# The corrected threshold of each score group, made by VectorE instead of GpSimd

## What is computed

```python
dots = jnp.einsum('bhid,bhjd->bhij', q, k) * QK_SCALE
dots = jnp.einsum('hg,bgij->bhij', W_pre_th, dots)        # heads are mixed
dots = jnp.where(causal[None, None], mask_value, dots)
top = jax.lax.top_k(dots, TOPK)[0]                        # TOPK = 64
vk = top[..., -1:]
dots = jnp.where(dots < vk, mask_value, dots)
attn = jax.nn.softmax(dots, axis=-1)
attn = jnp.einsum('hg,bgij->bhij', W_post_th, attn)       # and mixed again
out = jnp.einsum('bhij,bhjd->bhid', attn, v)
```

## Time and profile before

| | |
|---|---|
| median of three runs | 2098.49 us |
| the profiled execution | 2098.69 us, span 2096.9 us |
| PE busy | 1952.4 us, 93% of the span |
| VectorE busy | 1668.8 us, 80% |
| ScalarE busy | 1612.7 us, 77% |
| GpSimd busy | 862.8 us, 41% |
| granted TensorE clock, mean | 0.981 |

### The profile page before, as it was taken

The page is one execution under the profiler, slowest core; times in us unless marked ns, Lnnn a source line. Parts: engine busy times, 40 slices in busy tenths (PEclk is TensorE's granted clock), DMA queues, the critical chain, the costliest instruction groups (busy, mean ns, idle before and its releaser), DMA issues. The chain is left out here.

```text
span 2096.9 us, 56133 instructions
## 1 busy us (share of the span) xinstructions
PE 1952.4 (93%) x16059; PEld 1292.3 (62%) x16060; DVE 1668.8 (80%) x7716; ACT 1612.7 (77%) x4412; POOL 862.8 (41%) x2675
## 2 busy tenths in 40 slices
PE   7996789999999999999999999999999999996997
PEld 3433456676667666766676677666766776674433
DVE  6355389978997899789978997999699969985335
ACT  4553489978997899789968996899689978963554
POOL 3000454455445544554454445544554455421000
PEclk9997899999999999999999999999999999998998
DMA  5002012301230222122211221122112211213002
GB/s 170 26 1 95 12 33 53 79 18 45 61 73 18 62 55 60 26 54 68 45 33 48 68 48 29 48 68 48 29 48 68 48 26 46 66 45 95 0 1 80
DMA packets 113228, 104.78 MB, mean 50 GB/s; under 512 B 34449, under 2 KB 110865, under 8 KB 112913
## 3 DMA queue, kind: packets, MB, share of 16 engines
q1 hardware_dynamic: 108000, 96.65, 18.6%
q10 hardware_dynamic: 4912, 4.46, 0.7%
HBM read 19.14 MB, written 12.71 MB: 15 GB/s over the span
## 5 line engine op out<-in xcount | busy, mean ns | idle before, releaser
L1076 PEld LDWEIGHTS bankC<-R,E 128*128 128x128 f32 x2560 | 319.9, 192 | 49.7 <-issue 17.6
L1060 PE MATMUL bankB<-raw,mixpre 128*128 128x76 f32 (+37 forms) x1024 | 334.5, 421 | 13.6 <-DMA raw<-SC 12.3
L1076 PE MATMUL bankC<-R,E 128*128 128x128 f32 x2560 | 333.9, 277 | 11.5 <-POOL R L1452 11.5
L1557 DVE TENSOR_SCALAR_CACHE_REDUCE S<-S,minus_thr 128x68 f32<-128x68 f32 (+56 forms) x456 | 232.9, 511 | 110.9 <-POOL minus_thr L1436 110.1
L1427 POOL TENSOR_TENSOR S<-S,diagmask 128x8 f32<-128x8 f32 x512 | 120.2, 238 | 395.4 <-ACT S L1284 360.4
L1284 ACT ACTIVATE S<-bankB,aim_first 128x68 f32<-128x68 f32 (+56 forms) x456 | 227.3, 506 | 57.8 <-PE bankB L1060 56.9
L1452 POOL TENSOR_SCALAR R<-mixpost,rinv 128x128 f32<-128x128 f32 x512 | 199.3, 402 | 101.1 <-DVE rinv L1591 99.0
L1310 ACT ACTIVATE E<-S,nmax 128x12 f32<-128x12 f32 (+56 forms) x512 | 238.8, 523 | 0.0
L1060 PEld LDWEIGHTS bankB<-raw,mixpre 128*128 128x128 f32 x1024 | 160.2, 190 | 119.0 <-issue 94.4
L1646 DVE SCALAR_TENSOR_TENSOR E<-S,limit,E 128x68 f32<-128x68 f32 (+56 forms) x456 | 221.8, 521 | 8.6 <-ACT E L1310 4.7
L1049 PE MATMUL bankD<-KT,QT 64*64 64x132 f32 (+8 forms) x2304 | 177.4, 401 | 43.3 <-ACT qk L1214 29.4
(11 more groups left out here) (187 smaller groups left out, 4188.7 us busy)
## 6 DMA issues: line engine op xcount, KB each, us to landing
X_first<-in_L_attn_x_dram ACTq DMA_DIRECT2D x8, 512.0 KB, 9.9
x<-X_first SPq DMA_DIRECT2D x8, 512.0 KB, 2.9
xt<-x SPq DMA_DIRECT2D x32, 128.0 KB, 2.4
x<-xt SPq DMA_DIRECT2D x32, 128.0 KB, 2.4
X_last<-x SPq DMA_DIRECT2D x8, 512.0 KB, 7.5
out_dram<-X_last SPq DMA_DIRECT2D x8, 512.0 KB, 2.9
raw<-SC SPq DMA_DIRECT2D x8, 258.0 KB, 5.3
raw<-SC SPq DMA_DIRECT2D x8, 254.0 KB, 4.8
```

What stands on the lines that cost most here:

```text
L1060: last = nc.tensor.matmul(bankB[n % 2][:, 0:wide(n)], W.mixpre[:, :], raw[n % RAWS][:, 0:wide(n)], start=True, stop=True)
L1076: last = nc.tensor.matmul(bankC[:, n % 2, jb * P:(jb + 1) * P], E[n % EBUFS][:, jb * P:(jb + 1) * P], R[n % RBUFS][:, :], start=True, stop ...
L1557: nc.vector.tensor_scalar(row, row, minus_thr[:, col(n)], None, ALU.add, ALU.max, accum_out=rmax[:, col(n)]).then_inc(max_done, 1)
```

## The change

GpSimd's function `threshold`, its buffer `moved` and the semaphores `thr_moved` and `thr_ready` are dropped. VectorE gets a function `threshold(n)`: it waits for the count of group n and makes `minus_thr` of this one column with one `tensor_scalar` (multiply by a column of `aim_slope`, add a column of `aim_base`). It is called for both ranked groups of a pair ahead of the row sweep of the first, and the row sweep waits for `tk` instead of `thr_ready`.

```diff
-            def threshold(ns):
-                cols, steps = ring(ns), in_batch(ns)
-                pool.wait_ge(below_done, ranked_upto(ns[-1]))
-                nc.gpsimd.tensor_tensor(moved[:, cols], below[:, cols], W.aim_slope[:, steps],
-                                        ALU.mult).then_inc(thr_moved, len(ns))
-                pool.wait_ge(thr_moved, ranked_upto(ns[-1]))
-                nc.gpsimd.tensor_tensor(minus_thr[:, cols], moved[:, cols], W.aim_base[:, steps],
-                                        ALU.add).then_inc(thr_ready, len(ns))
-
...
-                if ranked_in(n0):
-                    threshold(ranked_in(n0))
...
+            def threshold(n):
+                dve.wait_ge(below_done, ranked_upto(n))
+                at = step(nc.vector.tensor_scalar(minus_thr[:, col(n)], below[:, col(n)], W.aim_slope[:, group(n)],
+                                                  W.aim_base[:, group(n)], ALU.mult, ALU.add))
+                thr_at[n] = at
+
+            thr_at = {}
+
             def row_max(n):
...
                 if is_ranked(n):
-                    dve.wait_ge(thr_ready, ranked_upto(n))
+                    dve.wait_ge(tk, thr_at[n])
                     nc.vector.tensor_scalar(row, row, minus_thr[:, col(n)], None, ALU.add, ALU.max,
                                             accum_out=rmax[:, col(n)]).then_inc(max_done, 1)
...
                 more = 2 <= n0 and n0 + 2 < NG
+                for n in ranked_in(n0 + 2) if more else ():
+                    threshold(n)
                 if more:
                     row_max(n0 + 2)
```

More of the change, by code:

```diff
@@ L762, in attention_phase @@
         parts_ok = sb("parts_ok", [P, 1])
-        moved = sb("moved", [P, RING])
         minus_thr = sb("minus_thr", [P, RING])
@@ L800, in attention_phase @@
         below_done = sem("below_done")
-        thr_moved = sem("thr_moved")
-        thr_ready = sem("thr_ready")
         max_done = sem("max_done")
```

## The result

The changed kernel takes 2142.8 us in the median of five runs (2141.0 to 2146.4) beside 2098.5 us (2097.5 to 2099.5) of the kernel before: 1.0214 of it, 95% interval 1.020 to 1.0227. It is slower by 44 us. The forecast was slower by 11, with a range up to 2122, so the sign was right and the size was wrong by a factor of four.

What follows compares the result with a forecast made beforehand. PE was taken as the bound, with VectorE also full in each batch element's second half. 1.5 us for each of seven elements (10.5) plus 1.5 for the last, less 1, gave +11.0 us: 2109.5 us, range 2096.5 to 2122.

Steps and rivals of the forecast that it cites:

- The price of a pair: VectorE time for a pair's two new operations: 0.28 us from the `limit` row, 64 us for 228 pairs.
- the high end: Dearer price of 0.40 us a pair, 0.06 us per operation for a scalar column: 2123.5 us, chance 0.12.
- The lateness sum: VectorE's lateness followed pair by pair through each batch element's second half: 1.99 us late when R is made.
- 0.56 spare: At the pair at 1041.60, the first R ends 0.56 us before PE turns with it, absorbing that much lateness.
- It starts level at 956.34: At the third quarter's first pair VectorE carries no lateness; that pair then gives 0.28 - 0.55 = -0.27 us.
- Direct waits are not on PE's path: Nearly all of VectorE's 110 us of threshold waits lies where it is ahead of supply, not where PE waits.
- The two "faster" rivals: Shorter direct waits speed PE's chain, about 2092 us, chance 0.08; dropped GpSimd operations free VectorE, 2087 us, chance 0.03.
- A direct wait costs 0.3 us with VectorE: From count to sweep some 0.3 us instead of 0.83, so up to 0.5 us goes from each direct wait.
- GpSimd's relief is worth nothing: GpSimd loses 464 operations; R moves by about 0.1 us where GpSimd was behind, elsewhere not: zero.
- VectorE's spare is enough: Rival: low price, or PE's waits for ScalarE absorb the lateness; 2098.5 us within 4, chance 0.23.
- PE's waits for ScalarE may take up lateness, 1 us off: Last-quarter PE waits of 0.44 and 1.12 us might absorb part of the lateness; 1 us taken off overall.
- The signs named: Profile after: VectorE busy up 60 to 90 us, GpSimd down about 90 or more, PE's R waits above 11.5.

Runs made afterwards that it cites:

- the run with one less: The changed kernel with each new VectorE operation using one scalar column and a constant instead of two scalar columns: 2129.4 us (1.015).
- the run with GpSimd's operations kept: The changed kernel in which GpSimd still does its two threshold operations per pair, into a spare column nobody reads: 2144.6 us.
- wait first, one column: The changed kernel with the row sweep's wait on tk named first and one scalar column less per new operation: 2107.8 us (1.0046).
- wait first: The changed kernel with the row sweep's wait on tk named ahead of those on masked and nmax_ready, same instructions: 2125.6 us (1.0127).
- The run of the operations added: The kernel before, with VectorE also doing the new operations into an unread column while GpSimd still makes the threshold: 2124.4 us (1.0128).
- the change up to group 25: The change made only for groups up to 25 of each batch element, the others keeping GpSimd's two operations: 2099.3 us (1.0003).
- the shorter GpSimd chain: The kernel before, threshold still on GpSimd but with one operation per group, started at that group's count: 2099.2 us (1.0001).
- the like edit at the cut of E: The kernel before with the wait on tk named first instead of last at VectorE's cut of E: 2097.6 us (0.9993).

## Why the prediction failed in size and held in kind

**The price of a pair (0.28 taken, 0.42 measured) is the term that failed.** What was mis-sized are the scalar columns. The prediction counted one for each operation, 0.06 us, at the high end only, and none in the value taken. The operation has two, and the run with one less shows 0.062 us for it. The pair `limit`, taken as the nearest row, has none: its cut starts 0.133 us after the first `limit` record of 0.149 ends, 0.28 in all. The new record is 0.266, and the sweep follows 0.157 us after its end, 0.42 in all.

The prediction also put the sweep's wait on `tk` at nothing ("replaced one for one"). Where VectorE is full, `thr_ready` had been raised before the sweep came up, so that the sweep starts 0.05 us behind `flip` in the earlier trace rows. `tk` is raised by an operation that VectorE has only just begun, and named last that wait costs 0.06 us (0.238 against 0.182). The row of `limit` holds a wait of this kind, so its 0.28 had the wait in it, and I read it as the price of the operations alone. The high end of 0.40 was near the truth.

**The lateness sum was the right mechanism.** With 0.42 in the prediction's own steps it gives -0.13 + 2.94 + 0.84 - 1.10 + 1.26 = 3.8 us, less 0.56 spare: 3.3 us for a batch element. The lengths of batch elements, from the first reciprocal of one to the first of the next, allow a check. They are middle ones. The clock falls some 20 us ahead of the end of an element and its cost lands in the next one (see below), so each row has only those with no such fall ahead of them. For the changed kernel that is a single one; the run with GpSimd's operations kept has 210.2 too.

| | us a pair | length, us | longer by |
|---|---|---|---|
| kernel before | 0 | 205.6 to 206.5 | |
| wait first, one column | 0.25 | 206.7 to 207.2 | 0.9 |
| wait first | 0.37 | 208.5 to 208.9 | 2.8 |
| changed kernel | 0.42 | 210.2 | 4.3 |

By the same steps, 0.25 a pair gives -0.30 + 1.75 + 0.50 - 1.10 + 0.75 = 1.6, less 0.56, 1.0 us, and 0.37 gives 3.2 - 0.56 = 2.6. So the sum holds to some 0.2 us at the lower prices and misses 1.0 at the highest. (At the 0.31 a pair which the prediction mentions, its steps give some 3 us more in all, not 2.)

**PE waits for R at more places than the one in the sum.** In the second half of the batch element of the earlier trace rows the kernel before has no wait of PE for R, the changed kernel has four: 0.18 us at 989.92, 0.65 at 1003.51, 0.24 at 1049.53 and the 1.94 at 1063.77.

```profile
1003.51 0.71 PE L1073 MATMUL bankC<-R,E 128*128 128x128 f32 x4 [0.65 <-POOL R L1440]
```

The prediction had looked at how early R is at one place alone. Over the six middle batch elements such waits in the second half come to 2.6 to 3.3 us each in the changed kernel, to 1.9 to 2.2 with the wait first, and to 0.7 to 1.1 with one column less besides; in the kernel before none is there. So the lateness does reach PE through R. The elements are longer than these waits by some 1.3, 0.7 and 0.1 us, and where that lies isn't shown.

**"It starts level at 956.34" was wrong at 0.42.** In the kernel before, the sweep of the pair at 956.34 started 1.83 us after the count ended (954.31 + 0.20, ScalarE; rows of this place):

```profile
954.31 0.20 ACT L1294 ACTIVATION_READ_ACCUMULATOR junk_first<-S 128x1 f32 x1
```

In the changed kernel the same count and the same sweep (128x300):

```profile
971.38 0.20 ACT L1291 ACTIVATION_READ_ACCUMULATOR junk_first<-S 128x1 f32 x1
...
974.08 0.53 DVE L1551 TENSOR_SCALAR_CACHE_REDUCE S<-S,minus_thr 128x300 f32<-128x300 f32 x1
```

That is 2.50 us after it, 0.67 late where the prediction had -0.27 (-0.13 at 0.42 a pair). The lateness had begun in the second quarter: three pairs earlier the sweep started 2.51 us after the count where it had been 1.98. There I had called 4.3 us of idle time a cover without looking at which pairs it lay in. That is 0.8 of the 1.0 us that the sum misses at 0.42. But with the wait first the same sweep is 0.38 late where the steps have -0.18, and the whole sum for that price is off by 0.2 only. So its agreement at that price is in part luck.

**The clock was missing altogether.** In the attention stage from 290 us on (to 1890 in the kernel before, to about 1940 in the changed one) the kernel before never leaves 2.4 GHz. The changed kernel falls to 1.2 GHz eight times there, seven times for 3.4 us and once for 6.8, and the run with the wait first three times. The run of the operations added has two falls. What a fall costs can be read inside one trace: in the run with the wait first, the two batch elements behind a fall near 638 and 1475 us took 210.1 and 210.4 us, the other middle ones 208.5 to 208.9, so 1.6 us each. In the changed kernel five of them behind a fall took 211.3 to 212.0 and the one without 210.2, 1.1 to 1.8 more. Half of 3.4 us is 1.7, for a PE that is full. Nine such spans make about 14 us.

The parts add up for the two profiled executions, which are 47.7 us apart (2146.4 and 2098.7), more than the medians. It is 4.3 x 7 = 30 without the clock, and 14 from the clock. The last batch element took 205.9 us instead of 197.4, with three of the nine spans in it and one just ahead of it. Beyond these four, 6.4 us, some 2 us are its own, where I had allowed 1.5. That is 46 of the 47.7 us.

Point by point, the rest:
- *Direct waits are not on PE's path.* Right, shown in two runs: the change up to group 25 (1.0003) and the shorter GpSimd chain (1.0001). The 64 us less waiting in the changed kernel beside a loss are in keeping with it. The two "faster" rivals are out.
- *A direct wait costs 0.3 us with VectorE.* A little less: the sweep starts 0.22 us after the pair's second count ends (1359.00 + 0.20 in the rows below, and the same at the other such waits), where it was 0.83 with GpSimd. VectorE now waits at the count, 46.2 us in 31 times instead of 110.1 in 105.

```profile
1358.88 0.63 DVE L1538 TENSOR_SCALAR minus_thr<-below,aim_slope,aim_base 128x1 f32<-128x1 f32 x2 [0.79 <-ACT junk_first L1291]
1359.00 0.20 ACT L1291 ACTIVATION_READ_ACCUMULATOR junk_first<-S 128x1 f32 x1
1359.42 0.42 DVE L1551 TENSOR_SCALAR_CACHE_REDUCE S<-S,minus_thr 128x204 f32<-128x204 f32 x1
```

- *GpSimd's relief is worth nothing.* Right (2144.6 with the operations kept).
- *VectorE's spare is enough.* Wrong for the change, and still 9 us short at 0.25 us a pair (2107.8).
- *PE's waits for ScalarE may take up lateness, 1 us off.* Not seen: 0.44 and 1.12 us stand in the changed kernel unchanged, at 1073.87 and 1078.79, moved along with PE, as the text had suspected.
- *The signs named.* VectorE's busy time rose by 96.1 us (60 to 90 was written), GpSimd's fell by 117.5 (90 or more), and PE's waits for R grew, most of it in the last quarter of each batch element.

What stays open: why the clock falls behind some waits and not behind others (below), and how the time splits to better than some 2 us between lateness and clock. That the lateness reaches PE through R is read from PE's waits. A version with R earlier by one pair would test it directly and wasn't run.

## What to carry to other kernels

An engine that is 88% busy on average can be 96% busy for half the time. Cost an added instruction there at its full start-to-start time, and carry the lateness from pair to pair against the time by which its result used to be early, at every place where that result is needed, and over the quiet stretch ahead too. Build the price of a small operation from all of its parts, every scalar column and the wait of what comes next, and name first the wait that is due last: in the changed kernel that alone was worth 17 us, while the like edit at the cut of E in the kernel before was worth nothing. A long list of waits on an engine is no gain in store unless the engine behind it waits as well.

## What the runs showed of the hardware

- **A second scalar column costs VectorE 0.06 us.** Start to start, a one-column `tensor_scalar` takes 0.186 us with two scalar columns and 0.124 with one (records of 0.266 and 0.207). `flip`, without any, takes 0.05, but it is another operation (two columns of int32), so the price of the first is an estimate from that row.
- **The place of a wait costs 0.06 to 0.12 us.** The wait named first rides on the instruction, the others stand in a semaphore instruction of its own in the queue. With the wait for the engine's own earlier result in the latter, the next operation starts 0.157 us after the end of that result's record, which is 0.238 after the start of the second operation with two scalar columns and 0.240 with one. With it in the former it starts after 0.182 and 0.121, as if nothing waited (0.181 where nothing did).
- **The clock can fall behind a wait of under 2 us, and need not.** In the run with the wait first, PE waited 1.81 us for R at 637.12 and 1.72 at 1473.36, and the granted clock fell to 1.2 GHz about a microsecond later; behind waits of 1.73 us at 847.26 and 1055.96 it stayed at 2.4. In all four PE was busy again at once. In the changed kernel a wait of 1.94 us at 641.87 has no fall behind it and one of 1.94 at 852.11 has. The rows of the run with the wait named first at two of these places, from its timeline of PE and then from its table by stretch (the last numbers are PEclk, DMA share and GB/s), the first with a fall, the second without:

```profile
637.12 2.63 PE L1073 MATMUL bankC<-R,E 128*128 128x128 f32 x16 [1.81 <-POOL R L1440]
...
847.26 2.05 PE L1073 MATMUL bankC<-R,E 128*128 128x128 f32 x16 [1.73 <-POOL R L1440]
```

```profile
638.00:642.00 4.00, 4.00 (x24) 4.00 (x23) 3.99 (x26) 1.61 (x3) 0.67 (x4) 0.57 0.02 4
...
848.00:852.00 4.00, 4.00 (x38) 4.00 (x38) 3.99 (x26) 2.62 (x9) 0.81 (x4) 1.00 0.00 0
```

The same kind of wait stands ahead of both stretches, PE is busy in all of both, and what tells them apart isn't shown by any run. So a kernel whose PE is full but for one such wait loses 1.6 us or nothing. And the loss of time grows faster than the price: from 0.37 to 0.42 us a pair (the run with the wait first and the changed kernel) the time grew by 17 us, by 20 between the profiled executions. The longer batch elements explain 1.5 x 7 = 10 of these, and six more spans at 1.2 GHz the other 10.
